# A graph network kernel: eleven node steps moved from the message stage into the second softmax

## What is computed

```
x = layernorm(x + L0(x))    # attention over the edges: per-edge scores, softmax over equal dst, weighted sum, @ W_out
x = layernorm(x + L1(x))    # q, k, v, softmax over equal dst, then beta = sigmoid([out, x_r, out-x_r] @ Wbeta.T),
                            # (beta*x_r + (1-beta)*out) @ W_m2n.T
```

## Time and profile before

| | us |
|---|---|
| median of 3 runs | 1377.34 |
| lowest, highest | 1364.89, 1383.67 |
| the profiled execution | 1366.76 |
| its span | 1365.0 |
| PE busy | 1197.2 (88%) |
| DVE busy | 1039.6 (76%) |
| ACT busy | 810.9 (59%) |
| POOL busy | 842.9 (62%) |

### The profile page before, as it was taken

How to read it: one execution, slowest core, us unless ns; L and a number is a source line. 1 busy time by engine, 2 the same in 40 slices (tenths; PEclk the granted TensorE clock), 3 DMA queues, 4 the chain that set the end, 5 groups by cost and what they waited for, 6 DMA issues and landing times. The chain is left out here.

```text
span 1365.0 us, 29010 instructions
## 1 busy us (share of the span) xinstructions
PE 1197.2 (88%) x7386; PEld 1061.5 (78%) x7386; DVE 1039.6 (76%) x3852; ACT 810.9 (59%) x2583; POOL 842.9 (62%) x1060
## 2 busy tenths in 40 slices
PE   3799999999995889899896999999999992988881
PEld 2688998989984777777775899999999982877771
DVE  3476777777779788898885888888888876877771
ACT  0366666666667756566565666666666675555652
POOL 4688888888843544455543666666666632377775
PEclk9899999999999999999999999999999996999996
DMA  6668888888853678787786766666666622555541
GB/s 161 193 186 262 285 253 274 264 272 264 268 185 116 185 228 238 236 246 240 240 243 202 222 209 198 192 201 197 199 197 185 200 93 98 158 176 169 172 155 58
DMA packets 208940, 277.09 MB, mean 203 GB/s; under 512 B 40060, under 2 KB 140563, under 8 KB 208777
## 3 DMA queue, kind: packets, MB, share of 16 engines
q1 hardware_dynamic: 188793, 224.13, 52.9%
q0 software_dynamic: 19264, 50.85, 13.1%
q10 hardware_dynamic: 720, 0.26, 0.1%
HBM read 159.73 MB, written 117.12 MB: 203 GB/s over the span
## 5 line engine op out<-in xcount | busy, mean ns | idle before, releaser
L744 PE MATMUL banks<-m_ext,node_XT 128*128 128x257 f32 x1568 | 377.9, 384 | 0.0
L744 PEld LDWEIGHTS banks<-m_ext,node_XT 128*128 128x128 f32 x1568 | 286.3, 193 | 32.9
L770 DVE SCALAR_TENSOR_TENSOR node_X<-banks,node_be,node_X 128x256 f32<-128x256 f32 x392 | 169.7, 474 | 79.2 <-ACT node_be L696 53.8
L671 POOL TENSOR_TENSOR node_r<-node_vv,half 128x4 f32<-128x4 f32 (+1 forms) x202 | 215.3, 1066 | 17.1 <-ACT node_X L683 0.3
L702 ACT ACTIVATE node_XT<-banks 128x512 f32<-128x512 f32 x196 | 117.2, 598 | 139.4 <-PE banks L734 125.2
L666 POOL TENSOR_SCALAR node_vv<-node_mv 128x4 f32<-128x4 f32 (+1 forms) x202 | 57.0, 282 | 212.4 <-DVE node_mv L778 196.9
L763 DVE BATCH_NORM_STATS2 node_st<-node_X 128x6 f32<-128x256 f32 x392 | 145.7, 413 | 20.7 <-DMA node_X<-in_x 19.3
L709 ACT ACTIVATE node_sq<-node_X 128x256 f32<-128x256 f32 x392 | 158.0, 409 | 0.0
L734 PE MATMUL banks<-ident,node_X 128*128 128x128 f32 x784 | 122.2, 279 | 28.5 <-DVE node_X L784 14.1
L683 ACT ACTIVATE node_X<-node_X,node_r 128x256 f32<-128x256 f32 x326 | 146.0, 496 | 1.4 <-POOL node_r L671 1.4
L824 POOL DMA_INDIRECT ring<-in_x,src_col x100 | 106.9, 1069 | 35.2 <-issue 14.2
(11 more groups left out here) (262 smaller groups left out, 2773.4 us busy)
## 6 DMA issues: line engine op xcount, KB each, us to landing
node_X<-in_x SPq DMA_DIRECT2D x196, 256.0 KB
out<-node_X SPq DMA_DIRECT2D x196, 256.0 KB
ring<-rows SPq DMA_DIRECT2D x300, 128.0 KB
rows<-ring SPq DMA_DIRECT2D x100, 256.0 KB
rows<-ring SPq DMA_DIRECT2D x200, 128.0 KB
MB<-keeps SPq DMA_DIRECT2D x40, 320.0 KB, 5.5
MB<-picks SPq DMA_DIRECT2D x50, 128.0 KB
MB<-in_src SPq DMA_DIRECT2D x25, 195.3 KB
```

The source lines that it names most:

```text
L671: pool.tensor_tensor(r[:, s % 4, NT * lo:NT * hi], v, self.c.half[:, NT * lo:NT * hi], ALU.pow).then_inc(self.roots, 1)
L744: last = pe.matmul(ps[:, NT * o + k, 0:D + 1], self.XT[:, o, k * D + h * P:k * D + (h + 1) * P], c.m_ext[:, h, :], start=(h == 0), stop=(h ...
L770: last = dve.scalar_tensor_tensor(out=X[:, n % U, k, :], in0=ps[:, b + k, 0:D], scalar=self.be[:, n % 4, k:k + 1], in1=X[:, n % U, k, :], ...
```

## The change

```
-NODE_SHARE = (74, 10, 66, 45, 10)
-NODE_NORMED = ["A" if 74 <= s < 84 or s >= 186 else "AD"[s % 2] if s >= 84 else "D" for s in range(NSTEPS)]
+NODE_SHARE = (74, 10, 66, 34, 21)
+NODE_NORMED = ["A" if 74 <= s < 84 or s >= 184 else "AD"[s % 2] if s >= 84 else "D" for s in range(NSTEPS)]
```

## The result

| | us |
|---|---|
| changed kernel, median of 20 runs | 1383.40 (1375.62 to 1404.77) |
| kernel before, beside it, median of 20 runs | 1370.05 (1364.89 to 1390.90) |
| ratio after / before | 1.0107, 95% interval 1.0085 to 1.0130 |
| the profiled execution after | 1376.1, span 1374.3 |

The change costs 1.1%, some 15 us (12 to 18). That is inside "no change that can be told", and inside the range, but the sum said +5 us. Some executions of either kernel, five of the 20 of the changed one, fell in a slower state of the device; the medians hold them, the ratio doesn't.

A forecast was written before the change was run, and what follows sets the result against it. PE bounds the message stage; soft2 has no full engine and is a chain through DVE, PE and ACT. -23.1 + 28.2 = +5.1 us, on the four-run mean of 1373.2 put at 1378 us, range 1361 to 1396.

The forecast's parts named there:

- Soft2, +28.2: Second softmax stage: the moved node entries at ACT's pace make it 65.3 us against 37.1, 28.2 us more.
- Entry 183: Soft2, ahead of the 14 full entries: its block is normalised by DVE; 2.15 to 3.13 us, taken as 2.5.
- step 2: Soft2, a softmax step beside ACT's work: costs nothing while ACT is the pace.
- the `Exp`: Soft2: with its two table loads it adds 3.7 us between sigmoids, 6.84 us apart instead of 3.13.
- step 9: Soft2, a softmax step on DVE behind a node entry: that entry takes 4.00 us, 0.9 us more.
- Message stage, -23.1: Message stage: PE-bound, gives back 23.1 us for the node entries taken out (bounds -26.1 and -20.8).
- The start: Message stage start: tile 0 no longer stands behind one entry's 4.30 us of matmuls; 2.0 us less (0 to 4.3).
- Ten entries at 2.18 and longer runs: Message stage from tile 0: ten fewer entries on PE, 21.8 us less; longer unbroken tile runs, 0.7 us more.
- Idle of soft2 fills up: Rival, chance 0.2: moved entries fill ACT's idle 11.6 us, soft2 grows only 22.8 us; sum -0.3, time 1373.
- SP's chain: Rival, chance 0.12: SP's store and load chain paces soft2, 3.48 us against ACT's 3.13; 3.5 us more, 1382.
- The lead of three entries: Soft2: stores issue about three entries, 9.4 us, before DVE needs the slot's next block, so SP's delay counts nothing.
- Half clock through soft2: Rival, chance 0.06: PE stays at 1.2 GHz and paces entries 184 to 199; 18.7 us more, 1397.

The follow-up runs named there:

- The new start in the kernel before: Kernel before with four node entries instead of three ahead of message tile 0 and one fewer between the tiles; 1374.49 us, ratio 1.0018.
- left_out: Against the kernel before, eleven node blocks left out of the computation: the new message stage with the old soft2; 1356.22 us, ratio 0.9886.
- share_only: Changed kernel with the old table of who normalises, so DVE normalises block 185 in soft2; 1381.94 us, ratio 1.0081 to the kernel before.

## Why the prediction came out as it did

The predicted time (1378, range 1361 to 1396, no change that can be told) held. The sum under it was +5.1 us and the traces give +12.5, the times +12 to +18. That is above the upper bound of the terms (+10.9), so the range held by its margin for scatter, and not by the sum. One of the signs came true by luck: the message stage was to end near 1096 and ended at 1094.6, but 8.1 of the 23.8 us by which this is earlier than before had passed ahead of the stage, and the second execution ended it at 1104.6. Step by step:

**Soft2, +28.2: right, and in the main for the reasons given** (measured +28.4, and 65.5 us for 65.3 on the sigmoids' own measure, 1094.77 to 1160.25). Entry 183: 2.35 (2.5). Sigmoid to sigmoid 3.13 us in the six periods from entry 188 to 194 (1109.86 to 1128.66). The four before them weren't 3.13 each: 3.32, 2.15, 3.51 and 3.76, together 12.7 for 12.5. In entry 187 ACT waited 0.51 us for the shift L757, which stands behind the scans of step 2 on DVE. The prediction had counted step 2 at nothing under ACT's work, and named a distance set by DVE as a sign of being wrong; here it was one period and half a us. Entries 184 to 197 with the `Exp` and step 9 among them: 49.4 (43.8 + 0.5 + 3.7 + 0.9 = 48.9). Of it the entry with the `Exp` is 6.93 us (7.3 forecast; in it a stall of 0.34 us at L757, forecast 0.5), and that with step 9 is 4.00 (4.03). Entry 197 took 3.82 instead of 3.13, which was not forecast: PE's transposes at half clock kept ACT waiting for 0.59 us. Then 2.15, 1.65 and 0.98 (2.15, 1.76, 1.0), and 8.94 us from step 13 to L1615 (8.96).

**Message stage, -23.1: mis-sized; it is -15.9.** Two of its terms failed. (A small slip beside it: with 0.4 to 1.0 for the longer runs the lower bound is -25.7, not -26.1.)

*The start: forecast -2.0, measured +3.0.* The prediction wrote that "the first matmuls at half clock are then the tile's", and yet counted a gain. I saw that n152 took 4.30 us at half clock ahead of tile 0 and asked how much of this would be saved. It was the other way round. The wait ahead of tile 0 is set by DMA and DVE. n152 stood in it, was nearly free (its matmuls held tile 0 back by 1.2 us beyond the time its rows were ready), and paid for the slow clock in place of tiles 0 and 1. Without it, two things happen. Tiles 0 and 1 run slow: from tile 0 to tile 2 it is 8.7 and 9.0 us where it was 7.2, with one node entry between them in both. And in the new order n151's DVE work stands between the statistics and the normalisation of tile 0's rows, which are ready 2.2 to 2.6 us later, so that tile 0 comes 1.0 to 1.5 us later in spite of a shorter queue on PE. The first is shown, by the extra products. The second is read from DVE's rows in after; no run took it alone. The new start in the kernel before doesn't show it, since its tile 0 was late for another reason, the loads of its rows. The bounds of that term (0 to 4.3 us of gain) were wrong too: they left no room for a loss, although the prediction had the mechanism of one in its own sentence.

On the clock the page of the Trainium skill on TensorE (Matmul & The Clock Gate, Part 1), which the prediction weighed only for soft2, bears on this place more: half speed is the default and work releases it. The rows agree: L1383 at 1.91 us behind 14.69 us of waiting, 1.03 with five products ahead of it.

*Ten entries at 2.18 and longer runs: forecast -21.8 + 0.7 = -21.1, measured -18.8 and -19.0.* The count and the 2.18 us were right. The longer runs cost about 2.9 us, not 0.7, in the executions of after; it is the wait for DVE's normalised rows, 3.5 us on the weight loads and 1.4 on the matmuls, where it was 0.5. The size scatters: left_out and share_only have after's order in this stage, take 336.0 and 335.9 us from tile 2 to the end, and so lost about 1.8. On the third chip hardly anything of it is there: from tile 2 on, the kernel with the extra products takes 334.7 us and the kernel before with n153 moved 355.7, 21.0 less for the same ten entries, the forecast to 0.1. What the trace shows is that the waits are mostly ahead of third tiles of a run. Third and fourth tiles are 37 now and were 17 before. What isn't: their trigger. In the row quoted above the chain was ACT's L1422 (935.81, half a us after the modelled end of L1391), DVE's L1439 waiting 1.04 us for it, and DVE's in-order L1473 behind that. Less ACT work didn't cure it, and on the third chip the longest wait of ACT for L1391 was 0.6 us and not 1.1. Whether PE's signal comes late, or its record is early, stays open.

**The rivals.** *Idle of soft2 fills up*: false from 10 entries on (2.6 us for each), but in part true below 8 (about 1.1 us), which is why the split of before is near the best. *SP's chain*: the drift is there, 3.49 us from store to store over five periods,

```profile
1103.45 0.45 SPq L651 DMA_DIRECT2D out<-node_X  x1
...
1120.90 0.38 SPq L651 DMA_DIRECT2D out<-node_X  x1
```

but no `bn_stats` waited for a DMA in soft2, and the sigmoids kept 3.13 us. The lead of three entries was enough. *Half clock through soft2*: false; at the rhythm of one entry in 3.13 us the products took 1.91 us up to the `Exp`. Behind it they fell to half clock for one entry and into a second:

```profile
1128.06 0.63 PE L734 MATMUL banks<-ident,node_X 128*128 128x128 f32 x4 [0.76 <-issue]
...
1132.11 1.90 PE L744 MATMUL banks<-m_ext,node_XT 128*128 128x257 f32 x8
1138.11 1.09 PE L734 MATMUL banks<-ident,node_X 128*128 128x128 f32 x4 [4.10 <-ACT node_X L715]
1138.99 3.63 PE L744 MATMUL banks<-m_ext,node_XT 128*128 128x257 f32 x8
1142.42 1.00 PE L734 MATMUL banks<-ident,node_X 128*128 128x128 f32 x4
```

This was behind a wait of 4.10 us. In share_only it fell inside soft2 too, for one entry, behind the wait of 2.36 us. A third of an entry's products are transposes by count (by time they are 0.44 of 2.18 us, a fifth; the prediction says a third of the work). With this mix and shorter waits the clock stayed up, against what the Trainium skill says of transposes (TensorE: Matmul & The Clock Gate, Part 4), as I had read it. On the table loads the row was the better guide: 1.28 us each, and the whole entry 6.93 us. By the Trainium skill's 2.66 us for a switch (ScalarE: Activation LUTs, "What ACT_TABLE_LOAD costs") two of them would have made it an estimated 9.

## What to carry to other kernels

Filler work threaded into a stage isn't worth the same everywhere. Between units of a full engine it costs its whole length. In a wait ahead of the first unit it costs little, as long as it fits in the wait, and where it runs just ahead of that unit it takes the slow clock on itself. So when filler is taken out, look first which pieces ran in the ramp (ran, not stood in the list), and what runs cold in their place. Read the marginal price of an entry from both stages at the point where the split is (here 2.18 us against 2.6), not from busy shares. And where a term's mechanism can turn a gain into a loss, its bounds must include the loss.

## What the hardware showed beside this

- Five products that nobody needs, in PE's wait ahead of a stage, went with a tile 2 that came 3 us earlier in a stage whose own work was unchanged; 2.1 to 2.4 of them lie between tile 0 and tile 2, where L1383 took 1.03 us instead of 1.91.
- In the soft2 of after the granted clock fell behind 4.10 us of waiting, and not in the 35 us before, in which PE was busy for 79%, with waits of 0.3 to 1.4 us before most entries. In that of share_only it fell behind a wait of 2.36 us.
- The chips differ by stage: on the third chip the output stage was 195 to 197 us, on the others 209 to 214, and soft2 with the ten entries of before was 37.3 us in all four executions, one of them on the third chip. What a stage costs may be compared from chip to chip where its length repeats like that, and not in the output stage.
